# Layer 0's two attentions leave their outputs by feature, with the softmax shares applied a stage later

## The chip, the cores and the metric

One core of one Trainium2 chip runs the whole program in one launch. The metric is device time in microseconds (us): the median of three runs. TensorE does matrix products and transposes, VectorE and ScalarE work on 128 partitions, GpSimd does small vector work, and DMAs are issued by the queues of SyncE, ScalarE and GpSimd. In the profile they are PE (with PEld for its weight loads), DVE, ACT, POOL and SP; a `q` behind the name is the engine's DMA queue.

## What is computed

Two transformer layers on x, 8 samples x 512 tokens x 320 features, with a context of 8 x 64 x 192. Only layer 0 is changed. With 20 heads of 16 features:

```python
def _attn(x, ctx, wq, wk, wv, wo, bo, heads):
    q, k, v = ...                       # heads x 16 features
    sim = jnp.einsum('bhid,bhjd->bhij', q, k) * scale
    a = jax.nn.softmax(sim, axis=-1)
    out = jnp.einsum('bhij,bhjd->bhid', a, v)
    return out.transpose(0, 2, 1, 3).reshape(b, n, heads * dh) @ wo + bo
x = _attn(ln(x), ln(x), ...) + x        # self-attention
x = _attn(ln(x), context, ...) + x      # cross-attention
a, g = split(ln(x) @ ff_w1 + ff_b1); x = a * gelu(g) @ ff_w2 + ff_b2 + x
```

Everything is fp32; a product is made exact enough from rounded high and low halves (names in `_hi`, `_lo`, `_tail`).

## The kernel before

`transformer` runs one stage after another: the opening with q, k and v (to 207.5 us of the profile), `self_attention` (to 701.8), `dense_phase` with main "q", which applies the attention's output weight, adds to x, normalises and makes the queries of cross-attention (to about 852), `cross_attention` (to 1028.9), `dense_phase` with main "ff" (to 1552), and then layer 1 (to the end at 3341), whose own functions are not changed and whose dense phases already take their input by feature (`by_feature=True`, tile `attn_T`). Each stage is one block of five instruction streams held together by counting semaphores; each engine works strictly in the order written, so a wait holds everything behind it. The next stage's first loads wait for the last stores of the stage before.

**Self-attention** works in 40 groups, each of 4 heads of one sample (5 groups a sample), in 8 units `j` of PE work: two score matmuls by query for the row maxima (`natural`, L1250, tile `nat`), two transposed score matmuls (`transposed`, L1259, tile `sT`), and products with v (L1277, tile `o_ps`). The maxima are DVE's (L1391, 16 a group), the exponentials ACT's (L1325). The maxima are cut into three bf16 parts by POOL (L1362 to L1365), turned by PE (L1267, `turn_shift`), copied by ACT (L1330) and sent by SP as four small DMAs into `q_stack` (L1211). SP also loads q and k (L1196, 12 DMAs a group) and v (L1237). A finished group is in `o_ps` as 4 heads x 32 rows (16 values, the softmax sum in row 16) by 512 tokens. ACT copies it to `o_sb` (L1318), PE turns it by four transposes in unit 2 (`turn_output`, L1287), ACT copies it to `o_turned` (L1334), DVE takes 16 reciprocals (L1385), POOL multiplies (L1352), and SP stores it by token (`self_out`, L1232).

**The dense phases** go through 8 samples, each engine by the list `body`, whose steps run `ahead` samples in front. `oT` turns the loaded attention output (12 transposes a sample, L848, from `attn_nat`, loads L691 and L695); ACT and DVE split it (L949 `oT_hi`, L1012 `oT_lo`); `oproj` multiplies (L326) and DVE adds it to `x_resid` (L1016); statistics and `z` follow (L1023, L1034). By feature, as in layer 1, `attn_T` is loaded by three DMAs (L677, L680) of which the first two blocks of 128 rows are one, and `oT` is the split alone. In the q stage the loop between samples goes over the single tile of the loaded input. In "ff", PE is occupied throughout by `ff1` and `ff2` (L326, L891), with the steps of the next sample between them.

**Cross-attention** also has 40 groups, each with 64 keys: `nat` L2017, `sT` L2026, shift turn L2034, `turn_output` L2052, products L2044 on PE; exp L2084, copy of the shift rows L2089, its two DMAs L2092 and the copy `o_sb` L2098 on ACT; maxima L2156, reciprocal L2132 and multiplication L2134 on DVE; parts L2116 to L2119 on POOL, which behind each of the first groups also converts weights of the next stage (`PoolLoader`, L246 to L271) and adds the output bias to x (`EarlyBias`, L306, the first 32 groups). SP loads q (L1963, three DMAs a group), k (L1953) and v (L1973) and stores (L2000).

## Time and profile before

| what | us |
|---|---|
| median of 3 runs | 3343.64 (3338.16 to 3344.39) |
| the profiled execution, device time | 3342.7 |
| its span | 3341.0 |
| self-attention, layer 0 | 207.5 to 701.8 |
| q-dense, layer 0 | 701.8 to 852 |
| cross-attention, layer 0 | 852 to 1028.9 |
| ff-dense, layer 0 | 1028.9 to 1552 |

The span is 1.7 us shorter than the device time of the same execution. The mean granted clock of TensorE was 0.841 of full speed. A timeline row is one instruction or a run of equal ones; in brackets stands the idle time of the engine before it and what ended it.

### The profile page before, as it was taken

Reading aid. Unit: us, or ns where it says so; the run is one execution under the profiler, and the core shown is the slowest. Engines: PE = TensorE matmul, PEld = TensorE weight load, DVE = VectorE, ACT = ScalarE, POOL = GpSimd, SP = SyncE. Lnnn points to the kernel's source line nnn. Section 1 sums busy time; section 2 is a strip of 40 time slices with the busy share of each in tenths; the row PEclk is TensorE's granted clock in tenths of the full one; section 3 lists DMA queues with packets and bytes.
Section 4 is the critical chain, followed back from the end, with each engine's and each line's share of the span. In section 5 each row is a group of like instructions: output and inputs, shape, how many; then the busy total and the mean of one; then the engine's idle time right before and its main releaser. Section 6 shows DMA issues by size and latency. Waiting matters only on the chain. (4 is left out here: it accounts for less than half of the span.)

```text
span 3341.0 us, 47964 instructions
## 1 busy us (share of the span) xinstructions
PE 2936.9 (88%) x15594; PEld 1775.7 (53%) x15594; DVE 2157.7 (65%) x3834; ACT 1892.4 (57%) x3214; POOL 805.5 (24%) x1149
## 2 busy tenths in 40 slices
PE   6989999978696999998959999879978577899999
PEld 5754444457455888886731111111126342788888
DVE  5668888837453444444649999968868685444443
ACT  4328888844353232233549999989975355333322
POOL 2021221114640000000027888200003471200000
PEclk9969999989798999998975555555559898899999
DMA  8663333336762000001567557266723213010000
GB/s 228 211 166 101 106 107 103 90 80 158 165 176 46 10 10 19 9 0 38 152 173 163 128 137 164 32 90 83 97 56 96 79 45 92 26 36 18 25 17 16
DMA packets 358243, 296.57 MB, mean 89 GB/s; under 512 B 175602, under 2 KB 281914, under 8 KB 358058
## 3 DMA queue, kind: packets, MB, share of 16 engines
q1 hardware_dynamic: 347994, 273.93, 34.0%
q0 software_dynamic: 7280, 18.07, 2.1%
q10 hardware_dynamic: 2784, 2.29, 0.4%
q8 instruction: 94, 1.54, 0.2%
q14 instruction: 91, 0.75, 0.1%
HBM read 177.53 MB, written 114.52 MB: 87 GB/s over the span
## 5 line engine op out<-in xcount | busy, mean ns | idle before, releaser
L1591 PE MATMUL nat<-k_stack,q_stack 48*128 48x512 bf16 x640 | 381.0, 605 | 71.5 <-DMA k_stack<-k1w 31.1
L1391 DVE TENSOR_REDUCE neg_max<-nat 128x1 f32<-128x512 f32 x640 | 400.7, 682 | 61.3 <-PE nat L1250 61.2
L1625 DVE TENSOR_REDUCE m_all<-nat 128x1 f32<-128x512 f32 x640 | 423.3, 691 | 18.1 <-PE nat L1591 17.8
L804 POOL TENSOR_TENSOR rstd<-var_eps,neghalf 128x4 f32<-128x4 f32 x48 | 51.9, 1081 | 1588.0 <-DVE var_eps L1028 1588.0
L1645 ACT ACTIVATE nat<-nat,m_all 128x512 f32<-128x512 f32 x640 | 427.7, 2130 | 3.0 <-DVE m_all L1625 2.9
L1645 ACT ACTIVATION_READ_ACCUMULATOR nat<-nat,m_all 128x1 f32 x640 | 403.6, 1674 | 0.0
L1054 DVE SCALAR_TENSOR_TENSOR ff<-outp,bias,gel 128x512 f32<-128x512 f32 x160 | 120.1, 751 | 417.6 <-PE outp L326 417.6
L1325 ACT ACTIVATE probs<-sT 128x1024 f32<-128x1024 f32 x320 | 328.0, 1027 | 93.1 <-PE sT L1259 85.5
L968 ACT ACTIVATE gel<-outp,bias 128x512 f32<-128x512 f32 x160 | 110.0, 688 | 351.6 <-PE outp L326 351.6
L1839 ACT ACTIVATE exps<-sT 128x1024 f32<-128x1024 f32 x320 | 293.4, 1573 | 10.5 <-PE sT L1788 10.5
L972 ACT CAST ff_hi<-ff 128x512 fp32r<-128x512 f32 x160 | 99.2, 620 | 312.3 <-DVE ff L1054 312.3
L1591 PEld LDWEIGHTS nat<-k_stack,q_stack 48*128 48x128 bf16 x640 | 64.1, 102 | 387.9 <-ACT nat L1645 350.8
L1876 DVE TENSOR_SCALAR probs<-exps 128x1024 bf16<-128x1024 f32 x320 | 218.3, 692 | 67.8 <-ACT exps L1839 67.8
L1788 PE MATMUL sT<-q_stack,k_stack 51*128 51x512 bf16 x640 | 194.2, 604 | 34.6 <-DMA q_stack<-shift_rows 12.2
L1250 PE MATMUL nat<-k_stack,q_stack 48*128 48x512 f32 x640 | 200.8, 524 | 20.1 <-DMA k_stack<-k_hi 11.7
L1277 PE MATMUL o_ps<-probs,v_stack 128*32 128x256 f32 x2560 | 199.8, 394 | 1.1 <-issue 1.1
L1057 DVE TENSOR_TENSOR ff_lo<-ff,ff_hi 128x512 fp32r<-128x512 f32 x160 | 122.1, 763 | 109.7 <-ACT ff_hi L972 109.7
L1048 DVE TENSOR_TENSOR hT_lo<-h,hT_hi 128x512 fp32r<-128x512 f32 x144 | 111.6, 780 | 106.0 <-ACT hT_hi L963 105.7
L1250 PEld LDWEIGHTS nat<-k_stack,q_stack 48*128 48x128 f32 x640 | 80.0, 193 | 163.6 <-DVE neg_max L1391 129.2
L1259 PE MATMUL sT<-q_stack,k_stack 51*128 51x512 f32 x640 | 157.7, 430 | 0.5 <-ACT probs L1325 0.2
L1788 PEld LDWEIGHTS sT<-q_stack,k_stack 51*128 51x128 bf16 x640 | 34.0, 102 | 184.0 <-ACT exps L1839 165.7
L326 PE MATMUL outp<-hT_hi,Wff_hi 128*128 128x512 f32 x320 | 125.9, 393 | 4.6 <-DVE hT_lo L1048 4.6
(561 smaller groups left out, 7163.3 us busy)
## 6 DMA issues: line engine op xcount, KB each, us to landing
v<-vpad SPq DMA_DIRECT2D x64, 320.0 KB, 2.8
q_stack<-q_part SPq DMA_DIRECT2D x90, 160.0 KB, 5.8
k_stack<-k1w SPq DMA_DIRECT2D x90, 160.0 KB, 10.5
q_stack<-q_hi SPq DMA_DIRECT2D x160, 64.0 KB, 2.5
v_stack<-v SPq DMA_DIRECT2D x40, 256.0 KB, 3.2
q_stack<-q_hi SPq DMA_DIRECT2D x80, 128.0 KB, 2.8
raw<-v SPq DMA_DIRECT2D x16, 640.0 KB, 14.9
k_stack<-k_hi SPq DMA_DIRECT2D x158, 64.0 KB, 2.2
```

The costliest lines, as they stand in the source:

```text
L326: mm = pe.matmul(out, stay, move, start=(n == 0), stop=(n == len(terms) - 1))
L1250: pe.matmul(nat[(16 * n + t) % 3][:, :], q_stack[half, n % RING, pr, qt * P:(qt + 1) * P], k_stack[half, n % RING, pr, :], start=True, sto ...
L1259: mm = pe.matmul(sT[use % 2][:, ab, :], k_stack[half, n % RING, pr, kt * P:(kt + 1) * P], q_stack[half, n % RING, pr, :], start=True, stop ...
L1277: mm = pe.matmul(o_ps[VCOL * h:VCOL * h + VCOL, tok], v_stack[:, n % 2, kt, VCOL * h:VCOL * h + VCOL], probs[:, n % 2, h, kt, tok], start= ...
L1325: act.activation(probs[:, n % 2, 2 * pr:2 * pr + 2, kt, :], sT[use % 2][:, :, :], ACT.Exp, scale=DH ** -0.5).then_inc(s["a_turn_free"], 1)
L1391: dve.tensor_reduce(neg_max[:, n % 2, qt, 2 * pr + ab:2 * pr + ab + 1], nat[(16 * (n + 2) + t) % 3][:, :], AX.X, ALU.max, negate=True).the ...
L1591: pe.matmul(bank[i % NAT][:, :], q_stack[half, slot, g, pr, qt * P:(qt + 1) * P], k_stack[half, slot, g, pr, :], start=True, stop=True).th ...
L1625: dve.tensor_reduce(k.m_all[:, column(i // TILES, i % TILES)], bank[i % NAT][:, :], AX.X, ALU.max, negate=True).then_inc(s["e_max_ready"], 1)
L1645: act.activation(b[:, :], b[:, :], ACT.Exp, bias=k.m_all[:, col], accum_out=k.s_all[:, col]).then_inc(s["a_nat_free"], 1)
L1788: mm = pe.matmul(sT[u % TURNS][:, ab, :], k_stack[half, slot, g, pr, kt * P:(kt + 1) * P], q_stack[half, slot, g, pr, :], start=True, stop ...
L1839: act.activation(exps[:, u % EXPS], sT[u % TURNS][:, :, :], ACT.Exp).then_inc(s["a_turn_free"], 1)
L1876: dve.tensor_scalar(probs[:, u % KEPT], exps[:, u % EXPS], ROUND, -ROUND, ALU.add, ALU.add).then_inc(s["e_rounded"], 1)
```

## The change

In layer 0, both attentions store `o_ps` as it is: [128 x 512] per group, 4 heads x 32 rows, sums included and not divided (256 KB in place of 128 KB). `turn_output`, the second copy and the per-group reciprocal and multiplication are gone; the first copy is ACT's in self-attention and DVE's in cross-attention, into two buffers. Once a sample, SP loads the 20 rows of sums as [80 x 128], DVE inverts them, (self-attention only) POOL splits the result into halves, and SP stores these shares. The dense phases load the undivided output by heads (rows 0 to 15 of each 32): heads 0 to 7, heads 8 to 15, and heads 16 to 19 twice. New steps `scale` multiply it by the shares: in q, PE spreads the 20 shares over the features by one matmul a block into the banks that the transposes had, and DVE multiplies in place, three samples ahead; in ff, the shares are loaded broadcast to all features (8 DMAs a sample in place of 5) and DVE multiplies one sample ahead. The 12 transposes a sample are gone in both. The tile is free for the next load when `oT_lo` is done, where it was free after the transposes.

In cross-attention also: queries are loaded for two groups at once (three DMAs for two groups), the shift rows go in one DMA in place of two, POOL converts weights on every fourth group only and only those of the output and the first part of `ff_w2` (the second part is converted in the ff stage), and the bias is added in the last 32 groups in place of the first 32.

```diff
+            ahead = {"oT": 1, "oproj": 1, "stats": 1, "norm": 1, "zT": 1, "tail": -1, "scale": 1}
+            between = [[("tail", 0), *scale], oT[0:2], oT[2:], oproj[0:2], oproj[2:], [("stats", 0)], [("norm", 0)],
                        zT[0:2], zT[2:], []]
             body = []
...
+            if scale:
+                ahead["scale"] = 3
...
+                    zT[0], zT[1], oproj[1], zT[2], *scale[0:2], oproj[2], *scale[2:], oproj[3]]
...
+            if scale and main == "ff":
+                n_attn, shares = 8, sb("shares", [P, 3, TOK])
+            elif scale:
+                n_attn, shares = 5, sb("shares", [2 * HEADS, TOK], F32R)
+                spread = sb("spread", [2 * HEADS, ZCOL], F32R)
...
+                    if scale:
+                        heads = rows(attn_in, b * (QUADS * P), QUADS * P).rearrange("(h c) t -> h c t", c=VCOL)[:, 0:DH, :]
+                        loads = [(attn, heads)]
+                        if main == "ff":
+                            shared = rows(recips, b * HEADS, HEADS).unsqueeze(1).broadcast_to([HEADS, DH, TOK])
+                            loads.append((shares, shared))
+                        else:
+                            sp.dma_start(words(shares[:, :]), rows(recips, b * (2 * HEADS), 2 * HEADS)
+                                         ).then_inc(s["attn_in_loaded"], 16)
+                        for tile, src in loads:
+                            for c in range(2):
+                                sp.dma_start(tile[:, c, :], src[8 * c:8 * c + 8]).then_inc(s["attn_in_loaded"], 16)
+                            for half in range(2):
+                                sp.dma_start(tile[64 * half:64 * half + 64, 2, :], src[16:HEADS]
+                                             ).then_inc(s["attn_in_loaded"], 16)
...
+                if recips_stored:
+                    sp.wait_ge(s[recips_stored], s.before(recips_stored))
...
+                    if kind == "scale" and main != "ff":
...
+                        if m == 0:
+                            pe.wait_ge(s["attn_in_loaded"],
+                                       at["attn_in_loaded"] + b * (16 * n_attn) + 16 * n_attn)
+                        bank_free(pe, st, b)
+                        pe.matmul(bank_of(st, r)[:, :], spread[:, m * P:(m + 1) * P], shares[:, :], start=True, stop=True
+                                  ).then_inc(s[turned[st][0] + "_full"], 1)
...
+                    if kind == "scale":
...
+                        dve.tensor_tensor(attn[:, m, :], attn[:, m, :], share, ALU.mult).then_inc(s[done], 1)
...
+                    sums_of = rows(out, b * (QUADS * P), QUADS * P).rearrange("(h c) t -> h c t", c=VCOL)[:, DH, :]
+                    sp.dma_start(sums, sums_of.rearrange("h (x t) -> h x t", t=P)
+                                 ).then_inc(s["a_sums_loaded"], 16)
...
+                    wait(sp, "a_share_split", 2 * b + 2)
+                    for i, half in enumerate((share_hi, share_lo)):
+                        sp.dma_start(rows(recips, (2 * b + i) * HEADS, HEADS).rearrange("h (x t) -> h x t", t=P),
+                                     words(half)).then_inc(s["a_recip_stored"], 16)
...
+                        wait(sp, "a_o_copied", n - 1)
+                        sp.dma_start(rows(out, (n - 2) * P, P), o_sb[:, n % 2, :]).then_inc(s[f"a_o_stored{n % 2}"], 16)
+                    if exists(n - 3) and (n - 3) % QUADS == QUADS - 1:
+                        load_sums((n - 3) // QUADS)
+                    if exists(n - 6) and (n - 6) % QUADS == QUADS - 1:
+                        store_shares((n - 6) // QUADS)
                     if exists(n + 1):
                         wait(sp, "a_pv_done", n)
                         sp.dma_start(v_stack[:, (n + 1) % 2, :, :],
                                      rows(v, (n + 1) * TOK, TOK).rearrange("(t p) c -> p t c", p=P)
                                      ).then_inc(s[f"a_v_loaded{(n + 1) % 2}"], 16)
...
-                        if exists(n - 2) and j == 2:
-                            turn_output(n - 2)
...
                         wait(act, "a_pv_done", n - 1)
-                        wait(act, "a_turn_full", output_use(n - 3) + 1 if n > 2 else 0)
-                        act.copy(o_sb[:, :], o_ps[:, :]).then_inc(s["a_o_copied"], 1)
+                        wait(act, f"a_o_stored{n % 2}", 16 * (n // 2 - 1))
+                        act.copy(o_sb[:, n % 2, :], o_ps[:, :]).then_inc(s["a_o_copied"], 1)
...
-                        if exists(n - 2) and j == 2:
-                            wait(act, "a_turn_full", output_use(n - 2) + 1)
-                            wait(act, "a_o_normed", n - 3)
-                            act.copy(o_turned[:, n % 2, :], output_bank(n - 2)).then_inc(s["a_turn_free"], 1)
...
+                def split_shares(b):
+                    wait(pool, "a_recip", b + 1)
+                    wait(pool, "a_recip_stored", 32 * b)
+                    pool.tensor_copy(share_hi, shares).then_inc(s["a_share_split"], 1)
+                    wait(pool, "a_share_split", 2 * b + 1)
+                    pool.tensor_tensor(share_lo, shares, share_hi.bitcast(F32), ALU.subtract
+                                       ).then_inc(s["a_share_split"], 1)
...
-                    if n >= 4:
-                        norm(n - 4)
+                    if n > 2 * QUADS and n % QUADS == 1:
+                        split_shares(n // QUADS - 2)
...
+                def invert(b):
+                    wait(dve, "a_sums_loaded", 16 * (b + 1))
+                    wait(dve, "a_share_split", 2 * b)
+                    dve.reciprocal(shares, sums).then_inc(s["a_recip"], 1)
...
+                        if t == 8 and exists(n - 4) and (n - 4) % QUADS == QUADS - 1:
+                            invert((n - 4) // QUADS)
...
+                    wait(sp, "x_recip", b + 1)
+                    sp.dma_start(rows(recips, b * HEADS, HEADS).rearrange("h (x t) -> h x t", t=P), shares
+                                 ).then_inc(s["x_recip_stored"], 16)
...
-                    if exists(n - 1) and exists(n - 1 + RING):
+                    if exists(n - 1) and exists(n - 1 + RING) and n % 2 == 0:
                         wait(sp, "x_turn_free", uses["scores", n - 1] + 1)
-                        load_q(n - 1 + RING)
+                        load_q((n - 1 + RING) // 2)
                     if exists(n - 1) and n % PER == 0 and b - 1 + KEYS < BATCH:
+                        wait(sp, "x_turn_free", uses["scores", n - 1] + 1)
...
+                    if exists(n - 2):
+                        wait(sp, "x_o_copied", n - 1)
+                        sp.dma_start(rows(out, (n - 2) * P, P), o_sb[:, n % 2, :]).then_inc(s[f"x_o_stored{n % 2}"], 16)
+                    if exists(n - 3) and (n - 3) % PER == PER - 1:
+                        load_sums((n - 3) // PER)
+                    if exists(n - 5) and (n - 5) % PER == PER - 1:
+                        store_shares((n - 5) // PER)
...
-                    if exists(n - 2):
-                        turn_output(n - 2)
...
-                            act.dma_start(words(q_stack[QROWS:ROWS, (n + 2) % RING, pr, :]),
-                                          words(shift_sb[6 * pr:6 * pr + 6, n % 2, :])
-                                          ).then_inc(s[f"x_shift_loaded{n % 2}"], 16)
-                    if exists(n - 1):
-                        wait(act, "x_pv_done", n)
-                        wait(act, "x_o_turned", n - 1)
-                        act.copy(o_sb[:, :], o_ps[(n - 1) % 2][:, :]).then_inc(s["x_o_copied"], 1)
+                        act.dma_start(words(q_stack[QROWS:ROWS, (n + 2) % RING, :, :]), words(shift_sb[0:12, n % 2, :])
+                                      ).then_inc(s[f"x_shift_loaded{n % 2}"], 16)
...
-                    loader.turn(pool, n)
-                    if n < BATCH * TT:
-                        early.add(pool, n)
+                    if n % 4 == 3 and n // 4 <= len(loader.jobs):
+                        loader.turn(pool, n // 4)
+                    if n >= NQ - BATCH * TT:
+                        early.add(pool, n - (NQ - BATCH * TT))
...
-                def norm(n):
...
-                    dve.reciprocal(recip[:, r], o[:, :, :, DH]).then_inc(s["x_recip"], 1)
-                    wait(dve, "x_recip", n + 1)
-                    dve.tensor_tensor(o_nat[:, r], o[:, :, :, 0:DH],
-                                      recip[:, r].unsqueeze(3).broadcast_to([P, TT, 4, DH]), ALU.mult
-                                      ).then_inc(s["x_o_normed"], 1)
...
+                    wait(dve, "x_pv_done", n + 1)
+                    wait(dve, f"x_o_stored{n % 2}", 16 * (n // 2))
+                    dve.tensor_copy(o_sb[:, n % 2, :], o_ps[n % 2][:, :]).then_inc(s["x_o_copied"], 1)
+
+                def invert(b):
+                    wait(dve, "x_sums_loaded", 16 * (b + 1))
+                    wait(dve, "x_recip_stored", 16 * b)
+                    dve.reciprocal(shares, sums).then_inc(s["x_recip"], 1)
...
+            w2 = [Split(nc, s, own, "ff_w2", rows(w["ff_w2"], 0, 2 * P), over=wo)]
...
+            w2.append(Split(nc, s, own, "ff_w2", rows(w["ff_w2"], 2 * P, FF - 2 * P)))
             dense_phase(nc, s, k, 0, "ff", w["n3_g"], w["n3_b"], [w1, *w2], wo2, cross_out,
...
+                        ff_bias=(w["ff_b1"], w["ff_b2"]), next_weights=w2[1:], by_feature=True, recips=cross_shares,
```

## Rows read from the trace of the kernel before

**Rows 1.** The page: span, and busy time, share and instructions of each engine.
```profile
span 3341.0 us, 47964 instructions
...
PE 2936.9 (88%) x15594; PEld 1775.7 (53%) x15594; DVE 2157.7 (65%) x3834; ACT 1892.4 (57%) x3214; POOL 805.5 (24%) x1149
```

**Rows 2.** Windows: stretch, us, busy (x) of PE, PEld, DVE, ACT, POOL, PEclk, DMA, GB/s.
```profile
250.00:660.00 410.00, 399.42 (x3682) 168.37 (x3680) 359.14 (x603) 336.97 (x390) 78.22 (x207) 1.00 0.37 102
706.00:830.00 124.00, 104.96 (x595) 89.15 (x596) 89.19 (x195) 55.67 (x92) 44.24 (x58) 0.93 0.56 137
858.00:878.00 20.00, 13.59 (x56) 10.86 (x56) 7.85 (x12) 4.39 (x6) 13.75 (x32) 0.50 1.12 207
858.00:1010.00 152.00, 139.52 (x819) 83.53 (x820) 74.23 (x149) 73.53 (x109) 88.85 (x229) 0.89 0.71 170
1060.00:1552.00 492.00, 487.23 (x2632) 432.57 (x2632) 203.24 (x384) 145.41 (x226) 28.10 (x15) 0.99 0.05 10
```

**Rows 3.** Timeline of PE in self-attention of layer 0: start, us, what, xcount.
```profile
452.77 0.50 PE L1250 MATMUL nat<-k_stack,q_stack 48*128 48x512 f32 x2
...
453.65 0.63 PE L1287 MATMUL sT<-ident,o_sb 128*128 128x128 f32 x4
...
454.77 0.51 PE L1250 MATMUL nat<-k_stack,q_stack 48*128 48x512 f32 x2
...
456.01 0.54 PE L1250 MATMUL nat<-k_stack,q_stack 48*128 48x512 f32 x2
```

**Rows 4.** Timeline of DVE in the same stretch.
```profile
450.41 0.24 DVE L1385 RECIPROCAL recip<-o_turned 128x16 f32<-128x16 f32 x1
...
461.98 0.24 DVE L1385 RECIPROCAL recip<-o_turned 128x16 f32<-128x16 f32 x1
```

**Rows 5.** Groups, one period of self-attention: busy us, mean ns, idle before and releaser.
```profile
L1391 DVE TENSOR_REDUCE neg_max<-nat 128x1 f32<-128x512 f32 x17 | 10.7, 681 | 1.4 <-PE nat L1250 1.4
```

**Rows 6.** Timeline of all engines at the end of self-attention.
```profile
696.41 0.59 ACT L1318 COPY o_sb<-o_ps 128x512 f32<-128x512 f32 x1 [2.60 <-PE o_ps L1277]
...
701.84 2.09 SPq L691 DMA_DIRECT2D attn_nat<-self_out  x4
```

**Rows 7.** Timeline of DVE in the q-dense stage of layer 0.
```profile
749.98 0.49 DVE L1016 TENSOR_TENSOR x_resid<-x_resid,oproj 128x320 f32 x1 [0.31 <-PE oproj L326]
...
755.04 0.69 DVE L1012 TENSOR_TENSOR oT_lo<-oT,oT_hi 128x512 fp32r<-128x512 f32 x1 [0.17 <-ACT oT_hi L949]
755.65 2.66 DVE L1034 TENSOR_SCALAR z<-x_resid,mv,rstd 128x320 f32 x4
...
765.37 0.49 DVE L1016 TENSOR_TENSOR x_resid<-x_resid,oproj 128x320 f32 x1 [0.32 <-PE oproj L326]
```

**Rows 8.** DMA issues: xcount, KB each, median us from issue to landing.
```profile
attn_T<-self_out_T SPq DMA_DIRECT2D x8, 512.0 KB, 4.2
```

**Rows 9.** GB/s in 40 slices of 2826 to 2836 us, layer 1's ff-dense loading.
```profile
GB/s 0 0 57 106 57 369 385 377 426 393 393 271 189 102 26 1 1 2 2 1 1 0 1 1 2 7 6 4 4 9 100 139 126 96 70 80 41 79 109 254
```

**Rows 10.** Timeline of all engines in cross-attention of layer 0.
```profile
969.08 1.03 ACT L2084 ACTIVATE probs<-sT 128x1024 f32<-128x1024 f32 x1
...
969.30 0.66 PE L2052 MATMUL o_ps<-ident,o_sb 128*128 128x128 f32 x4
...
970.58 1.39 ACTq L2092 DMA_DIRECT2D q_stack<-shift_sb  x2
...
972.07 0.59 ACT L2098 COPY o_sb<-o_ps 128x512 f32<-128x512 f32 x1 [1.52 <-issue]
...
972.56 1.03 ACT L2084 ACTIVATE probs<-sT 128x1024 f32<-128x1024 f32 x1
```

**Rows 11.** Groups in the first 40 us of cross-attention.
```profile
L306 POOL TENSOR_TENSOR x_resid<-x_resid,early_bias 128x320 f32<-128x320 f32 x7 | 6.0, 857 | 0.0
```

**Rows 12.** Timeline of PE in the ff-dense stage of layer 0.
```profile
1132.52 1.04 PE L848 MATMUL misc<-ident,attn_nat 128*128 128x128 f32 x8
...
1138.81 0.60 PE L848 MATMUL misc<-ident,attn_nat 128*128 128x128 f32 x4
```

More of the change, by code:

```diff
@@ L523, in dense_phase @@
         has_o = wo is not None
+        scale = [("scale", m) for m in range(3)] if recips is not None else []
         oT, oproj, zT = ([(x, m) for m in range(n)] for x, n in (("oT", 3), ("oproj", TT), ("zT", 3)))
@@ L1904, in cross_attention @@
         shift_sb = sb("shift_sb", [32, 2, TOK], F32R)
-        o_sb, o_nat = sb("o_sb", [P, TOK]), sb("o_nat", [P, 2, TT, 4, DH])
-        recip = sb("recip", [P, 2, TT, 4])
+        o_sb = sb("o_sb", [P, 2, TOK])
+        sums, shares = (k.m_all[0:TT * HEADS, P * i:P * i + P] for i in range(2, 4))
         loader = PoolLoader(nc, s, ctx, next_weights, 160)
@@ L2113, in _ @@
                     wait(pool, "x_turn_full", uses["shift", n - 1] + 1 if n else 0)
-                    mine = neg_max[:, n % 4]
-                    one, two, three = (parts[:, :, i:12:3] for i in range(3))
+                    mine, left = (x.rearrange("p t (a r) -> p t a r", a=2) for x in (neg_max[:, n % 4], rest[:, :, :]))
+                    columns = parts[:, :, 0:12].rearrange("p t (a i r) -> p t a i r", a=2, i=3)
+                    one, two, three = (columns[:, :, :, i, :] for i in range(3))
@@ L2159, in _ @@
                     if exists(n - 2):
-                        norm(n - 2)
+                        copy(n - 2)
+                    if exists(n - 4) and (n - 4) % PER == PER - 1:
+                        invert((n - 4) // PER)
+                invert(BATCH - 1)
         for name, n in counts.items():
             s.passed(name, n)
-        s.retire(counts)
+        s.retire([name for name in counts if name != "x_recip_stored"])
         loader.passed()
```

187 lines of the change are left out of this document (88 added, 99 removed).

## The prediction

> **What bounds the kernel now.** I read the page first: PE is busy for 88% of the span [rows 1]. So the question at each stage is whether PE is the engine that ends last there, and the windows answer it [rows 2]. Self-attention has PE busy 399.42 of 410 us at full clock, with DVE behind it at 359.14. In ff-dense PE works 487.23 of 492 us. In q-dense it works 104.96 of 124, so something else takes turns with it. In cross-attention it works 139.52 of 152, at a clock of 0.50 in the first 20 us. What PE loses in the first, the third and the last of these stages shortens them; in q-dense the loop between samples has to be walked. Layer 1 (1552 to 3341 us) is untouched.
>
> **Self-attention.** PE loses four transposes a group. Units 2 and 3 hold the same work but for them: they begin at 452.77, 454.77 and 456.01, so 2.00 against 1.24 us, a difference of 0.76 [rows 3]. The period is 11.57 us, from one reciprocal on DVE to the next [rows 4]. The next engine is DVE: 17 maxima take 10.7 us, so the group's 16 take 10.1, and its idle time of 1.4 us is all spent waiting for PE's scores [rows 5]. So the period can't fall under 10.1 (1.5 saved), and at the other end it stays at 11.57, if SP with its 18 DMAs a group can go no faster. I take PE's own 0.76, which still leaves DVE 0.7 us of slack: 38 steady groups x 0.76 = 29 us. ACT loses one copy and POOL a multiplication, both hidden. DVE's 16-column reciprocal of 0.24 us [rows 4] becomes one of 128 columns a sample. No row shows that; it lies between the 0.24 of 16 columns and eight times this, 1.9. I take 0.9, half of it in DVE's slack: 8 of them cost 4 us. POOL's split lies beside PE's work. The end grows: today 5.4 us pass from the last `o_sb` copy to the next stage's first load [rows 6]; then come a store, a load of sums, an inversion, a split and two stores, a transfer more, but no transposes: +3. **Self-attention: -29 + 4 + 3 = -22** (0 to -35).
>
> **q-dense.** The period is 15.4 us: the last add of one sample starts at 749.98, of the next at 765.37 [rows 7]. What counts is a new loop. The tile is now free when `oT_lo` is done, at 755.73 (755.04 + 0.69) [rows 7], 5.2 us behind the end of the last add (750.47). Only then may SP load the sample after, and PE waits in order for it before `oproj` 2 and 3. From the first `scale` to the end of the last add I count one matmul, two rounds of 8 oproj matmuls and their adds, 3.7 us. The loop is 5.2 + D + 3.7 with D the time from free tile to loaded tile. DVE has 89.19 us of work in 124 [rows 2], 11.1 a period, and gets three multiplications like `oT_lo`'s 0.69: 13.2, less than 15.4. PE loses 12 transposes and gets 3 matmuls. So the period stays near 15.4 unless D is over 6.5.
>
> D has two ends. Layer 1 loads the same 768 KB by feature in three DMAs and its large one lands in 4.2 us [rows 8]; with two more issues before the last lands, D is 5.5, and the loop of 14.4 stays hidden. The other end follows from the shape: every load of the trace with this many bytes has 128 rows as its outermost dimension, these have 8, 8, 4 and 4 heads. If each is spread over no more DMA engines than it has heads, four engines get 16 + 16 + 16 + 16 = 64 rows of 2 KB. All 16 engines together reach 426 GB/s [rows 9], so one moves 27 GB/s and a row takes 0.077 us: 4.9 us, with 2.4 us of fixed time (4.2 less 768 KB at 426 GB/s) and one issue in front, D = 7.9. The loop is then 16.8 us. I take this end: rows 8 is a row for a transfer of another shape, and this is the step on which my number hangs. 7 rounds x 1.4 = 10; the first load lands 2.4 later and its multiplications stand ahead of the first split (+2); PE's lost transposes in the warm-up give back 2. **q-dense: +12** (-3 with the early end; up to +20).
>
> The Trainium skill, "DMA: Bandwidth & Descriptors", the section on why a DMA increments its semaphore by 16, says that the engines used are the largest number up to 16 that divides the slowest dimension of both sides, and that from a hardware queue they are the lowest-numbered ones. By that the loads would use 8, 8, 4 and 4 engines and q-dense would be at +12; by the row of layer 1 alone it would be at -3. No row of this profile shows the number of engines of a transfer, so it stays open here.
>
> **Cross-attention.** The period between exponentials is 3.48 us (969.08 to 972.56). Two cycles are this long. PE has no gap and has the transposes in it, 0.66 as modelled, with 0.58 from their start to that of the products. ACT's is exp 1.03, shift copy 0.56, two DMA issues 1.39 and `o_sb` copy 0.59, 3.5 in all [rows 10]. The change cuts both: ACT loses the copy and one issue (to about 2.3) and PE the 0.58, to 2.90. DVE exchanges 0.68 for a copy of about 0.69; it has 74.23 of 152 us [rows 2]. From the 12th group on, 28 groups x 0.58 = 16 us. In the first 11 groups POOL sets the pace, busy 13.75 of 20 us [rows 2], and the bias additions there, 7 in 40 us at 0.86 [rows 11], move to the end, where POOL has room; but DMA is overfull there too (share 1.12 [rows 2]), so I count only 5 us. SP issues 22 DMAs a sample for 28. The end is longer by a transfer, +3. **Cross-attention: -18** (-8 if DMA, at a share of 0.71 before [rows 2], holds the period near 3.2; -27 if the start gains fully).
>
> **ff-dense.** 8 + 4 transposes a sample lie in a full PE: four more take 1.04 - 0.60 = 0.44 us, 0.11 each, and 12 are 1.31 [rows 12]. Seven samples in the steady part: -9.2. DVE's three multiplications have cover: it works 203.24 of 492 us; if that were gone they would cost 2 us a sample. The POOL work moved here (POOL 28.10 of 492 [rows 2]) is hidden until `ff2` needs the weights in the first sample. The first sample has no cover: with few engines 128 rows x 0.077 = 9.9 us against some 5 today, and multiplications before the split: +7. **ff-dense: -2** (-9 with the early end).
>
> **Sum.** -22 + 12 - 18 - 2 = -30. It is made against the profiled execution, 3342.7 us, which is 0.9 under the median: 3312.7, or 3313.6 by the median. I say 3313.
>
> **Rivals.** (1) *The head-wise loads land early.* For it: rows 8, and the DMA share of 0.56 in q-dense. Against it: their shape. Then -22 - 3 - 18 - 9 = -52: 3291. (2) *Something other than PE holds the attentions.* In self-attention SP issues 18 DMAs in 11.57 us and waits for the maxima's shift in between, and DVE's new inversion waits for a load of sums in the middle of its maxima; if the period stays at 11.3, 38 x 0.5 = 19 us of the gain are gone: 3332. For it: DVE is at 88% [rows 2]. Against it: its idle time is all PE's doing. (3) *Slower than before: the clock falls in q-dense.* PE waits at every sample for a late load there, with 85% busy and a clock of 0.93 now [rows 2]. At 0.50, as in 858 to 878, its 105 x 0.93 = 98 us of full-speed work take 195: +71 on the 124, 41 us over before, 3384. It decides once the low level covers more than 30/71 = 0.42 of the stage. Against it: self-attention leaves the clock at 1.00, and a PE at 80% does not look like the idle starts at which 0.50 stands. (4) *The stages give back at their ends what they gain*: the chain of last store, load of sums, inversion and store of shares stands at two ends, where today 5.4 us pass [rows 6]; were it 15 us longer than I count at each, the time would be 3343, no change. Against it: its transfers are 40 KB and less, and rows 8 has 4.2 us for 512 KB.
>
> **How the numbers follow.** My case has 0.50 (its own range 3300 to 3325), rival 1 has 0.24, rival 2 has 0.14, rival 3 has 0.06, rival 4 has 0.06. The range leaves out the clock, and the deepest gains of self-attention together with early loads: 3284 to 3336. About 0.2%, 6.7 us, is what a measurement can tell from no change. My case, the early loads and most of rival 2 lie beyond it: faster 0.88, same 0.05, slower 0.07.
>
> **What would show it.** Right: starts of unit 2 and 3 in self-attention alike, period 10.8; a q-dense period of 16.8 with PE idle for `attn_T`; exponentials 2.9 apart; layer-0 ff samples without L848 on `attn_nat`. Wrong: a landing of `attn_T` in layer 0 near 4 us (then 3291), a self-attention period that stays over 11 with DVE or SP before it, a granted clock at 0.50 within q-dense.

## The result, and the profile after

The changed kernel takes 3377.15 us (median of four runs, 3369.85 to 3382.74) against 3343.68 us, the median of four runs of the kernel before: a ratio of 1.0102 (95% interval 1.0076 to 1.0129), 33 us slower, where 3313 had been forecast. Its profiled execution has a span of 3380.3 us. The page and the windows that answer to [rows 1] and [rows 2]:

```profile
span 3380.3 us, 46635 instructions
...
PE 2928.0 (87%) x15106; PEld 1756.9 (52%) x15106; DVE 2206.2 (65%) x3820; ACT 1853.1 (55%) x3134; POOL 789.0 (23%) x1125
```

```profile
250.00:640.00 390.00, 381.27 (x3571) 155.41 (x3571) 363.70 (x577) 321.56 (x357) 60.77 (x183) 1.00 0.42 123
700.00:830.00 130.00, 95.42 (x392) 74.05 (x392) 84.76 (x169) 45.86 (x75) 39.76 (x49) 0.78 0.35 110
940.00:960.00 20.00, 20.00 (x70) 10.49 (x70) 6.79 (x10) 5.92 (x8) 9.08 (x24) 0.52 0.76 170
1100.00:1580.00 480.00, 474.44 (x2520) 420.43 (x2521) 217.34 (x399) 146.61 (x226) 44.70 (x31) 0.99 0.07 22
```

PE is busy for 9 us less and the kernel is 39 us longer in this execution. The loss shows in the clock column: q-dense, at 0.93 before, is at 0.78 (the second of these rows), and cross-attention has stretches in which PE is busy without a gap at a clock near 0.50 (the third). The stages, each from the first load of one to the first load of the next:

| us | before | after | difference | forecast |
|---|---|---|---|---|
| opening, up to self-attention's first load | 200.2 | 196.0 | -4.2 | 0 |
| self-attention | 501.7 | 477.6 | -24.0 | -22 |
| q-dense | 150.8 | 206.3 | +55.5 | +12 |
| cross-attention | 176.2 | 184.6 | +8.4 | -18 |
| ff-dense | 522.7 | 523.9 | +1.1 | -2 |
| layer 1 | 1789.4 | 1791.9 | +2.5 | 0 |

The mark of 207.5 us at which the table ahead of the prediction begins self-attention lies 7.3 us behind that stage's first load. Between profiles of the same code there are a few us: layer 1 takes 1788.2 to 1793.5 us in all the runs of this document, and the unchanged self-attention of e6 below takes 500.1.

**Self-attention** gained what was forecast. ACT's `o_sb` copies in the timeline of the changed kernel are 10.89 us apart, for 11.57 [rows 4]:

```profile
446.04 0.58 ACT L1373 COPY o_sb<-o_ps 128x512 f32<-128x512 f32 x1
...
456.93 0.58 ACT L1373 COPY o_sb<-o_ps 128x512 f32<-128x512 f32 x1
```

The end of the stage, in the timeline of all engines, is 8.4 us from the last copy to the next stage's first load (5.4 before [rows 6]), and the reciprocal of 80 x 128 takes 0.95 us:

```profile
665.22 0.58 ACT L1373 COPY o_sb<-o_ps 128x512 f32<-128x512 f32 x1 [3.82 <-PE o_ps L1342]
...
670.48 0.95 DVE L1433 RECIPROCAL m_all<-m_all 80x128 f32<-80x128 f32 x1 [26.49 <-DMA m_all<-self_out]
...
673.65 0.30 SPq L692 DMA_DIRECT2D shares<-self_shares  x1
```

**q-dense** is where the time went. Its period, last add to last add, is 23.13 us for 15.4 [rows 7]; DVE's timeline:

```profile
746.71 0.49 DVE L1074 TENSOR_TENSOR x_resid<-x_resid,oproj 128x320 f32 x1 [1.87 <-PE oproj L326]
...
769.84 0.49 DVE L1074 TENSOR_TENSOR x_resid<-x_resid,oproj 128x320 f32 x1 [1.86 <-PE oproj L326]
```

The queue of SP asks for the next sample at 752.62, right behind `oT_lo`, and PE stands idle for 4.60 us before its first `scale` matmul, which starts at 763.09. These are SP's row and then PE's:

```profile
752.62 0.33 SPq L692 DMA_DIRECT2D shares<-self_shares  x1
```

```profile
753.68 0.31 PE L326 MATMUL oproj<-o_w_lo,oT_hi 128*128 128x320 f32 x1
753.82 0.31 PE L326 MATMUL oproj<-o_w_hi,oT_lo 128*128 128x320 f32 x1
...
763.09 1.02 PE L887 MATMUL oT<-shares,spread 40*128 40x512 f32 x2 [4.60 <-DMA attn_T<-self_out]
...
764.46 0.47 PE L326 MATMUL oproj<-o_w_lo,oT_hi 128*128 128x320 f32 x1
764.73 0.47 PE L326 MATMUL oproj<-o_w_hi,oT_lo 128*128 128x320 f32 x1
```

So the time D of the prediction, from asking to loaded, is 10.5 us here, and 9.7 to 10.5 over the six loads of the steady part. Behind the wait the same pair of oproj matmuls is spaced by 0.27 us where it was 0.14 before the wait: the clock's lower level, 1.2 for 2.4 GHz. The loop reads 5.4 + 10.5 + 7.2 = 23.1.

The seven periods of the stage are 21.0, 22.7, 23.1, 22.9, 22.7, 22.8 and, with no load left in it, 14.9 us: together 42.8 us more than before. Another 11.4 us are lost ahead of them, from the stage's first load to the last add of the first sample: 29.3 us (673.65 to 702.99), for 17.9 before (701.84 to 719.73). The end is 1.3 us longer. DVE's rows, after and before:

```profile
702.99 0.49 DVE L1074 TENSOR_TENSOR x_resid<-x_resid,oproj 128x320 f32<-128x320 f32 x1 [1.74 <-PE oproj L326]
```

```profile
719.73 0.49 DVE L1016 TENSOR_TENSOR x_resid<-x_resid,oproj 128x320 f32<-128x320 f32 x1 [0.68 <-PE oproj L326]
```

**Cross-attention** takes 12.4 us more in the part that was to gain most. From the 12th exponential to the 40th and last it takes 108.8 us, for 96.4 before. Up to the 12th it gains 5.3 us, counted from the stage's first load, and its end is 1.3 us longer. ACT's rows, after and before:

```profile
945.88 1.02 ACT L2145 ACTIVATE probs<-sT 128x1024 f32<-128x1024 f32 x1 [3.67 <-PE sT L2095]
...
1054.70 1.02 ACT L2145 ACTIVATE probs<-sT 128x1024 f32<-128x1024 f32 x1 [2.09 <-PE sT L2095]
```

```profile
923.84 1.02 ACT L2084 ACTIVATE probs<-sT 128x1024 f32<-128x1024 f32 x1
...
1020.29 1.02 ACT L2084 ACTIVATE probs<-sT 128x1024 f32<-128x1024 f32 x1
```

**ff-dense** begins worse and runs better. Its first `ff1` product starts 40.9 us behind the stage's first load at 1064.57 in the changed kernel, and 33.0 us behind 1028.87 in the kernel before; what follows is 483.0 against 489.8 us. After, then before:

```profile
1105.46 0.79 PE L326 MATMUL outp<-hT_hi,w_hi 128*128 128x512 f32 x1 [3.71 <-DVE hT_lo L1106]
```

```profile
1061.83 0.80 PE L326 MATMUL outp<-hT_hi,w_hi 128*128 128x512 f32 x1 [3.42 <-DVE hT_lo L1048]
```

### The profile page after: what moved, and what is told of

It is laid out like the page before. It is cut to its first block and busy times, and to the rows that moved or that the text cites. A ratio compares the mean times of both kernels' runs of the same rounds, so it can differ in the third digit from the quotient of the medians.

```text
span 3380.3 us, 46635 instructions
## 1 busy us (share of the span) xinstructions
PE 2928.0 (87%) x15106; PEld 1756.9 (52%) x15106; DVE 2206.2 (65%) x3820; ACT 1853.1 (55%) x3134; POOL 789.0 (23%) x1125
## 5 line engine op out<-in xcount | busy, mean ns | idle before, releaser
L990 ACT CAST oT_hi<-attn_T 128x512 fp32r<-128x512 f32 x96 | 56.0, 618 | 151.2 <-PE oproj L326 83.8
L326 PE MATMUL outp<-hT_hi,w_hi 128*128 128x512 f32 x320 | 126.0, 394 | 4.9 <-DVE hT_lo L1106 3.7
```

The source lines that it names most:

```text
L326: mm = pe.matmul(out, stay, move, start=(n == 0), stop=(n == len(terms) - 1))
```

## The experiments

The expectations name their rival theories by letters. In the text below "theory D" is one of these, and D alone is the time of a load, from asking to loaded.

**1. Is it the shape of the load?** e1 loads contiguous blocks in q-dense (not the right rows, so the result is another one):

```diff
-    sp.dma_start(tile[:, c, :], src[8 * c:8 * c + 8])            # 8 heads x 16 rows
+    sp.dma_start(tile[:, c, :], rows(attn_in, b * 640 + 128 * c, 128))
```

> The changed kernel, but the q-dense stage loads its attention input as contiguous blocks of 128, 128, 64 and 64 rows in place of the gather by heads: the same bytes in the same number of DMAs, though not the right rows, so the result of layer 0 is another one. Theory A (the load by heads is slow because of its shape, and PE's waiting for it costs the clock too): the time from the free tile to the loaded one falls from 10.4 us to about 5.5, the period of the stage from 23.1 to 15 or 16, the stage from 206 us to 155 or less, the total by 45 to 50 us against the changed kernel, to some 3325. Theory B (any load into the one tile is that late, since it is asked for only when the tile is free and has five DMAs): the period stays over 21 and the total over 3360.

Measured: 3331.44 us (3325.68 to 3340.88), ratio to before 0.9975 (0.9962 to 0.9987); q-dense 162.5 us. In its timeline the load is asked for at 736.43 and the matmul that waits for it starts at 742.92, D = 6.5:

```profile
736.43 0.34 SPq L692 DMA_DIRECT2D shares<-self_shares  x1
...
742.92 0.72 PE L895 MATMUL oT<-shares,spread 40*128 40x512 f32 x2 [0.63 <-DMA attn_T<-self_out]
```

The period is 17.2 us. Theory B (over 21 us) is out. Theory A has the direction and most of the size: it had a D of about 5.5, a period of 15 or 16, a stage of 155 us or less and a total of some 3325. The transfers in 40 slices of 12 us, of the changed kernel from 752 and of e1 from 753, so that both loads are asked for some 0.7 us behind the first slice's start; first the busy share of the 16 DMA engines in tenths, then GB/s:

```profile
DMA  0092389894444454458999999997789874332222
GB/s 0 0 222 51 137 341 427 338 290 96 120 143 164 171 184 157 171 205 335 369 341 341 369 403 396 389 280 205 191 205 253 218 184 130 109 116 102 109 96 102
```

```profile
DMA  0097289899914999997799999999988610000000
GB/s 0 0 137 102 51 341 461 355 266 195 79 34 150 369 382 410 417 369 157 253 369 416 389 410 417 396 410 382 376 314 273 184 41 0 0 0 0 0 0 0
```

By heads, the mean busy share of the DMA engines falls to 4 and 5 tenths, at 96 to 205 GB/s, for nine slices, 2.7 us, in the middle of the load. It rises again behind the first stores of the queries (asked for from 756.44). In blocks the load runs at 7 to 9 tenths but for three slices. Gaps between the rows could do that as well as the outermost dimension of 8 and 4, so e8 keeps gaps and takes the small dimension away:

```diff
-    sp.dma_start(tile[:, c, :], src[8 * c:8 * c + 8])
+    sp.dma_start(tile[:, c, :], rows(attn_in, b * 640 + 256 * c, 256).rearrange("(p two) t -> p two t", two=2)[:, 0, :])
```

> The changed kernel, but q-dense loads every second row of the attention output: rows that don't lie together, as in the load by heads, but with 128 (or 64) rows as the outermost dimension where the load by heads has 8 (or 4) heads of 16. It leaves out the right rows, so layer 0's result is another one. If the outermost dimension decides how many DMA engines work, the load takes 6.5 us as with the contiguous blocks, the stage about 163 us, the total about 3331. If it is the gaps between the rows that make the load by heads slow, it takes 10.5 us, the stage 206 us and the total 3377.

```profile
739.46 0.34 SPq L692 DMA_DIRECT2D shares<-self_shares  x1
...
746.78 0.73 PE L897 MATMUL oT<-shares,spread 40*128 40x512 f32 x2 [1.45 <-DMA attn_T<-self_out]
```

D = 7.3, q-dense 169.4 us, the total 3336.75 (3325.01 to 3346.79), ratio 0.9977 (0.9964 to 0.9989). Over the six loads of the steady part D is 6.1 to 7.4 us in blocks (mean 6.6), 6.2 to 7.3 with gaps (7.0) and 9.7 to 10.5 by heads (10.0). So the gaps cost some 0.4 us (0.8 in the two loads shown), and the small outermost dimension some 3. The rule of the Trainium skill that the prediction weighed ("DMA: Bandwidth & Descriptors", "Why a DMA increments its semaphore by 16 and not by 1") fits this. The number of engines of a transfer is in no row here; what the rows show is the mean busy share of 0.4 to 0.5.

**2. Hide the load.** e2 gives q-dense two tiles and two semaphores, used in turn (SP's loop over the samples is written out for this):

```diff
+    attn2 = sb("attn_T2", [P, 3, TOK])
-    load_attn(b + early, b + (early - 1))     # waits for the split of the sample before
+    load_attn(b + early, b + (early - 2))     # of the one before that
```

> The changed kernel with two tiles for the attention input and the shares in the q-dense stage, so that the load of the next sample is asked for a sample earlier; loads by heads as they are. Theory A and B both say that the load is then hidden: period about 15.5, stage about 155 us, total about 3325. Theory C (not the wait for the load but the added matmuls and multiplications in the order of PE and DVE set the period): it stays near 20 and the total over 3355.

Measured: 3330.94 us (3321.73 to 3348.97), ratio 0.9966 (0.9950 to 0.9983). q-dense takes 165.9 us, 40 less than in the changed kernel. In its steady part the clock is 1.00 and DVE is busy for 85% of the window:

```profile
709.00:813.00 104.00, 83.35 (x438) 64.05 (x438) 88.87 (x177) 48.51 (x80) 43.73 (x54) 1.00 0.44 140
```

But the period is 17.3 us, not 15.5. DVE's rows, then PE's:

```profile
747.55 0.49 DVE L1091 TENSOR_TENSOR x_resid<-x_resid,oproj 128x320 f32 x1 [0.47 <-PE oproj L327]
...
764.85 0.49 DVE L1091 TENSOR_TENSOR x_resid<-x_resid,oproj 128x320 f32 x1 [0.49 <-PE oproj L327]
```

```profile
745.54 0.49 PE L904 MATMUL oT<-shares,spread 40*128 40x512 f32 x1 [1.32 <-DVE attn_T L1081]
...
752.62 0.44 PE L327 MATMUL outp<-hT_hi,q_hi 128*64 128x512 f32 x1 [1.57 <-DVE st_lo L1145]
```

With the load hidden, 1.9 us a sample of loss remain. PE stands 1.32 us before the third `scale` matmul, which needs the bank that DVE drains behind its `hT_lo`, and 1.57 us before the third q product. So theory C has a part, a small one. In e1 the period is 17.2 us too: with D at 6.5 the load no longer sets it alone.

**3. Cross-attention: which edit makes PE wait?** In the changed kernel the shift rows are PE's one large wait in the steady part of the stage, 15.3 us in 10 waits (view of the waits, from 895 to 1060); in the kernel before they were 2.2 us:

```profile
PE sT L2095 <- DMA q_stack<-shift_sb: 15.3, 10, 4.6
```

In PE's timeline one such wait of 2.27 us is followed by 24 us at the low clock, where a group takes 5.3 us; at 965.35 the `sT` matmuls are back at 0.68:

```profile
936.57 1.11 PE L2086 MATMUL nat<-k_stack,q_stack 96*128 96x128 f32 x8
939.95 0.74 PE L2095 MATMUL sT<-q_stack,k_stack 102*128 102x512 f32 x2 [2.27 <-DMA q_stack<-shift_sb]
...
942.91 1.97 PE L2086 MATMUL nat<-k_stack,q_stack 96*128 96x128 f32 x8
...
948.21 1.97 PE L2086 MATMUL nat<-k_stack,q_stack 96*128 96x128 f32 x8
...
965.35 0.68 PE L2095 MATMUL sT<-q_stack,k_stack 102*128 102x512 f32 x2
```

e3 takes back the loads for two groups, at the start of the stage as well as in its steady part:

```diff
-    def load_q(pair):     # 3 DMAs of 256 KB for two groups
+    def load_q(n):        # 3 DMAs of 128 KB a group
```

> The changed kernel with the queries of cross-attention loaded for one group at a time, three DMAs a group, as in the kernel before. Theory D (the loads for two groups, 256 KB each, stand before the shift rows on the DMA engines, PE waits for these and its clock drops after the wait): PE's 15.3 us of waiting for shift rows fall under 4, the stage goes from 184.6 to about 160 us, the total from 3377 to about 3352. Theory E (the clock drops in cross-attention because of the slow q-dense stage before it, or PE's own load): the stage stays within 5 us of 184.6.

```profile
PE sT L2094 <- DMA q_stack<-shift_sb: 5.2, 6, 1.7
```

Measured: the wait falls to 5.2 us, cross-attention to 166.3 us, the total to 3364.26 (3362.97 to 3368.76), ratio 1.0072 (1.0056 to 1.0089). Theory D had under 4 us, about 160 and about 3352, so it has the direction and part of the size; and the total by itself shows nothing, for the changed kernel taken once more (e11 below) has the same ratio, 1.0072. The table below settles the waits. e4 takes back the single shift DMA, and with it the order of the maxima in it:

```diff
-    act.dma_start(words(q_stack[QROWS:ROWS, (n + 2) % RING, :, :]), words(shift_sb[0:12, n % 2, :]))
+    for pr in range(2):
+        act.dma_start(words(q_stack[QROWS:ROWS, (n + 2) % RING, pr, :]), words(shift_sb[6 * pr:6 * pr + 6, n % 2, :]))
```

> The changed kernel with the shift rows of cross-attention sent as two DMAs of 6 rows, as in the kernel before. Theory F (one DMA of 12 rows lands later than two of 6): PE's waiting for shift rows falls from 15.3 us to under 5 and the total by 15 us or more. Theory D (they wait behind the loads of queries in either form): the wait stays at 10 to 20 us and the total within 8 us of the changed kernel's 3377.

Measured: 3379.05 us (3373.41 to 3392.42), ratio 1.0121 (1.0094 to 1.0149). The same within the spread, with 24.3 us of waiting for shift rows: theory F is out, the one DMA is no worse than two. All the profiles together, for this stage:

| queries loaded by | kernels | PE's waits for shift rows, us | first exponential behind the stage's first load, us | stage, us |
|---|---|---|---|---|
| 256 KB | changed, e1, e2, e4, e6, e8, e11 | 15.3, 16.3, 13.5, 24.3, 17.9, 15.6, 19.4 | 22.0 to 25.0 | 184.6, 169.1, 186.7, 178.1, 168.1, 178.1, 170.4 |
| 128 KB | e3, e5, e9, e10, e12 | 5.2, 3.7, 2.2, 2.4, 6.4 | 16.2 to 18.0 | 166.3, 159.2, 163.5, 164.2, 152.0 |
| 128 KB, stage as before | before, e7 | 2.2, 1.4 | 19.8, 19.1 | 176.2, 177.5 |

The waits go with the size of the loads in every kernel. That the shift rows, which are asked for on ACT's queue, stand behind these loads on the DMA engines is the likely reason, but no row shows their order. The bigger loads have a second price: the first exponential comes 4 to 9 us later. Of e3's 18 us, 8 lie ahead of the 12th exponential. The slow q-dense stage of theory E is out as well: in e1, e2 and e8 q-dense takes 162.5 to 169.4 us, and cross-attention still 169.1 to 186.7. How long the stage takes does not follow the sum of the waits: e2 has the fewest of the first row and the longest stage, with a mean clock of 0.74 from 856 to 1022 us.

**4. The parts alone.** e6 has only cross-attention and ff-dense of the change, e7 only self-attention and q-dense, with e2's two tiles:

```diff
# e6
-    self_attention(nc, s, k, q0, k0, v0, self_out, self_shares, [wq, wo], w["o1_b"])
+    self_attention_before(nc, s, k, q0, k0, v0, self_out, [wq, wo], w["o1_b"])
# e7
-    cross_attention(nc, s, k, q20, k20, v20, cross_out, cross_shares, [wo2, *w2], w["o2_b"])
+    cross_attention_before(nc, s, k, q20, k20, v20, cross_out, [wo2, *w2], w["o2_b"])
```

> Only the part of the change in cross-attention and ff-dense; self-attention and q-dense as in the kernel before. If cross-attention's loss is its own (queries by two groups before the shift rows), its stage takes 175 to 187 us against 176.2 and ff-dense 524 against 522.7: total 3340 to 3353, within 0.3% of before. If the drop of the clock in cross-attention comes from the slow q-dense stage before it, the stage takes 155 to 165 us and the total is 3322 to 3330.

> Only the part in self-attention and q-dense, with two tiles for the attention input; cross-attention and ff-dense as in the kernel before. Self-attention -27, q-dense +15 (a period of 17.3 against 15.4 and the later start), cross-attention 176 and ff-dense 523 as before: 3329, about 12 us faster. Rival (what self-attention gains comes back in q-dense's start and in layer 1): within 3 us of before.

e6: 3335.44 us (3330.29 to 3351.61), ratio 0.9982 (0.9968 to 0.9995); cross-attention 168.1 us, with 17.9 us of waiting for shift rows behind a q-dense stage of 151.5 us. This lies between the two forecasts: the waits are cross-attention's own, and what they cost differs from run to run (its spread is 21 us). e7: 3337.05 us (3332.35 to 3343.72), ratio 0.9977 (0.9966 to 0.9988), with 480.7, 165.0, 177.5 and 523.7 us in the four stages. That is 6 us under the kernel before, between the forecast of 12 and the rival's 3 at most. The profiled run, 4 us slower than the median, has self-attention 6 us over its forecast of -27 and layer 1 4 us longer (1793.5 for 1789.4), which is the same code.

**5. Both repairs, and what is left.** e5 is e2 and e3 together.

> The changed kernel with both repairs: two tiles for the attention input in q-dense, and queries of cross-attention loaded for one group at a time. Theory: the two losses lie in different stages and add up; q-dense 166 us and cross-attention 166 us as in the two runs alone, self-attention 467, together some 13 to 20 us under the double-tile kernel's 3331: 3311 to 3318, faster than the kernel before by about 25 us. Rival (cross-attention's clock depends on the stage before it, so with a full q-dense it drops anyway): cross-attention stays near 185 us and the total near 3330.

Measured: 3322.70 us (3316.79 to 3333.05), ratio 0.9943 (0.9928 to 0.9958), 5 us over the forecast range, with q-dense at 166.2 us and cross-attention at 159.2 in the profiled run. The rival (cross-attention near 185) is out, and the ratio is lower than with either repair alone, though its interval still touches e2's. Against the kernel before, cross-attention gains its 17 us ahead of the 12th exponential; from there to the last it takes 96.2 us for 96.4. DVE, PE and ACT of e5 show the next stall:

```profile
907.99 0.95 DVE L2209 RECIPROCAL m_all<-m_all 80x128 f32<-80x128 f32 x1 [3.96 <-DMA m_all<-cross_out]
```

```profile
909.63 1.64 PE L2103 MATMUL nat<-k_stack,q_stack 96*128 96x128 f32 x8 [2.42 <-DVE neg_max L2229]
```

```profile
902.86 1.03 ACT L2162 ACTIVATE probs<-sT 128x1024 f32<-128x1024 f32 x1 [1.42 <-PE sT L2112]
...
905.76 1.02 ACT L2162 ACTIVATE probs<-sT 128x1024 f32<-128x1024 f32 x1 [1.42 <-PE sT L2112]
...
912.27 1.02 ACT L2162 ACTIVATE probs<-sT 128x1024 f32<-128x1024 f32 x1 [5.03 <-PE sT L2112]
...
917.57 1.02 ACT L2162 ACTIVATE probs<-sT 128x1024 f32<-128x1024 f32 x1 [3.83 <-PE sT L2112]
```

DVE stands 3.96 us for the sums ahead of its maxima, PE 2.42 us behind it, and the exponentials, 2.90 us apart until then, come at 6.5 and 5.3. e9 puts the inversion one group later, and the store of the shares too:

```diff
-    if exists(n - 4) and (n - 4) % PER == PER - 1:
-        invert((n - 4) // PER)
+    if exists(n - 5) and (n - 5) % PER == PER - 1:
+        invert((n - 5) // PER)
```

> The kernel with both repairs and, in cross-attention, the inversion of the sums one group later on DVE (and the store of the shares one group later on SP). Theory G: with both repairs what is left of cross-attention's stalls comes from DVE waiting 4 us for the sums ahead of its maxima, PE waiting 2.4 us behind it, and the clock then at 0.50 for three groups of 5.3 us. Without that wait the two long stretches at 5.3 go, cross-attention falls from 159 to 145 to 152 us and the total from 3323 to 3308 to 3316. Rival H: the clock falls by itself whatever PE waits for; the 5.3 us stretches stay and the stage is 155 to 165 us.

Measured: 3319.05 us (3310.31 to 3320.39), ratio 0.9908 (0.9888 to 0.9928). PE's waits for the maxima are gone (0.4 us), but stretches at 5.3 us were still there in the profiled run (163.5 us for the stage, where theory G had 145 to 152), behind waits of 1.4 and 1.5 us for others. Theories G and H each have a part; how often the clock falls is not settled.

e10 asks what the 1.9 us a sample in q-dense are. It is e5 with multiplications that cover 8 of 512 columns:

```diff
-    dve.tensor_tensor(mine, mine, share, ALU.mult)
+    dve.tensor_tensor(mine[:, 0:8], mine[:, 0:8], share[:, 0:8], ALU.mult)
```

> The kernel with both repairs, where the three multiplications by the shares in q-dense cover 8 of 512 columns; it leaves the other columns undivided, so its result is another one. Theory I: DVE's three full multiplications (2.1 us a sample) are on the path that sets q-dense's period of 17.3 us; without them it is 15.2 to 15.5 and the stage 150 to 153 us for 166, the total 13 to 16 us under 3323. Rival J (PE's added matmuls and their order set the period): it stays over 16.8 and the stage over 162.

```profile
746.24 0.49 DVE L1091 TENSOR_TENSOR x_resid<-x_resid,oproj 128x320 f32 x1 [1.32 <-PE oproj L327]
...
763.01 0.49 DVE L1091 TENSOR_TENSOR x_resid<-x_resid,oproj 128x320 f32 x1 [1.33 <-PE oproj L327]
```

Measured: 3317.13 us (3314.38 to 3321.72), ratio 0.9918 (0.9897 to 0.9939); the period is 16.77 us, the stage 162.1. Theory I is out, and rival J holds but for 0.03 us. The multiplications are 0.5 of the 1.9 us; the order of PE's queue is the larger suspect, so e12 moves the third scale step behind the last product, on top of e9:

```diff
-    zT[2], *scale[0:2], oproj[2], *scale[2:], oproj[3]]
+    zT[2], *scale[0:2], oproj[2], oproj[3], *scale[2:]]
```

> The kernel with both repairs and the later inversion, and in q-dense the third scale step moved behind the last oproj step, so that PE does not stand before that product until VectorE has drained the bank of the first scale step. Theory K (the order of PE's queue, 1.3 us of waiting at the third scale matmul, is the larger part of what is left of q-dense's loss): the period falls from 17.3 to about 16.0 us, the stage from 165 to about 156 us, the total from 3319 to about 3310. Rival L (VectorE's own chain sets the period, it only gets the same work in another order): the period stays over 16.9 and the total within 4 us of 3319.

```profile
727.07 0.88 DVE L1091 TENSOR_TENSOR x_resid<-x_resid,oproj 128x320 f32 x2
...
743.40 0.88 DVE L1091 TENSOR_TENSOR x_resid<-x_resid,oproj 128x320 f32 x2
```

The period is 16.33 us (743.40 - 727.07 in DVE's timeline), the stage 162.2: the wait was worth 1.0 us a sample, between theory K's forecast and rival L's. The stage gained only 2.9 us for K's 9: its seven periods are 4.4 us shorter together, and its end, behind the last add, is 1.9 us longer. The total is 3308.86 us (3304.47 to 3313.08), ratio 0.9905 (0.9888 to 0.9921). Against e9's ratio of 0.9908, taken on another chip, the total can't tell the two apart, and e12's profiled run owes most of its lead over e9's to cross-attention (152.0 us for 163.5), which the edit leaves alone. Against the kernel before, both are 0.9% faster. They are the best complete versions here: the change with two tiles in q-dense, single-group query loads and the later inversion.

Last, the changed kernel itself again:

> The changed kernel itself once more, on the chip of the two kernels above. Every theory: 3370 to 3383, q-dense at 206 us; what varies from run to run is how long cross-attention spends at the low clock.

Measured: 3368.65 us (3366.83 to 3374.92), ratio 1.0072 (1.0050 to 1.0094), 1 us under the forecast range, with 203.5 us in q-dense and 170.4 in cross-attention, 14 less than in the first profile. So +8.4 for cross-attention in the first table is one draw from a range of about -6 to +8; with e1, e2 and e8, which have the same code there, -7 to +10.

## Why the prediction was wrong

**Self-attention: right.** The transposes were worth 0.68 us a group for 0.76, the end cost +3.0 as forecast, and the reciprocal is 0.95 us for 0.9. -24 for -22. DVE kept slack, as forecast: from 300 to 600 us its waits for PE's scores are 17.6 us, for 37.7 before.

**q-dense: right mechanism, badly sized, and this step alone turns the sign.** The forecast loop of 5.2 + 7.9 + 3.7 = 16.8 us measured 5.4 + 10.5 + 7.2 = 23.1. Three terms were short, in the loop shown:
- *D = 7.9.* The loads in the warm-up, with no stores of queries beside them, took 8.6 and 8.9 us (asked for at 687.54, matmul at 696.15). Within the loop the stores of the queries are asked for 4 us behind the load, and D was 10.5. The working had counted the load's own rows alone. That the stores make the difference is likely; no run took them away. The working also has a slip: its 4.2 us are the landing of a transfer of 512 KB [rows 8], from which it takes the time of 768 KB. With 512 KB its fixed time is 3.0 us and its D 8.5, near the warm-up's.
- *From scale to the last add, 3.7.* At full clock it is 5.2 us (e1: 742.92 to 748.13, the end of the last add). The text had counted one matmul and two rounds of products; all three scale matmuls lie in this stretch, and the third waits until DVE has drained the first one's bank, 0.62 us in e1 and 1.32 in e2.
- *The clock.* Another 2.0 us a sample (7.2 for e1's 5.2): PE, made to wait 3.9 to 4.6 us a sample, ran the products behind the wait at the low level. Rival 3 named this mechanism and the place, and had it at 0.06; "a PE at 80% does not look like the idle starts" was the sentence that failed. The stage's mean clock was 0.76, where it was 0.90 in the kernel before and in e1 and e2, not the 0.50 that the rival priced. If the clock has only the levels 0.5 and 1, a mean of 0.76 is the low one for 0.48 of the stage, an estimate, and that is over the 0.42 at which the rival was to decide. But 3384 is near the result by luck, by another sum: most of the loss is the waiting itself.

Together with 0.2 ahead of the asking these are 6.3 us in the loop shown. Over the stage the difference of +55.5 and +12 is 43.5 us: some 33 in the seven periods (+42.8 for +10), 9 ahead of the first sample's last add, where the second load is waited for in the same way (+11.4 for some +2), and 1.3 at the end. e1 and e2 take 44 and 40 us of the stage back. "So the period stays near 15.4 unless D is over 6.5" was wrong by itself, too: with D hidden it is 17.3. Of these 1.9 us, 0.5 go with the multiplications (e10) and 1.0 with the third scale step (e12). No run has both edits, so it is not shown that the two add up; if they do, 0.4 is left open.

**Cross-attention: the step that failed is "From the 12th group on, 28 groups x 0.58 = 16 us".** An undisturbed group did fall to 2.90 us as forecast (902.86 to 905.76 in e5), but these 28 groups cost 12.4 us in place of gaining 16. The shift rows are now due in 2 groups of 2.9 us and not of 3.48, and with loads of 256 KB beside them PE waits 15.3 us for them, where the text had costed this edit at nothing, beside the gain on SP's queue. And a wait can be followed by 10 to 27 us at the low clock, 2.4 us a group, which no term held. e3 shows the first cause, e5 the second one's other source, DVE's wait for the sums, which rival 2 had named for self-attention, where it did not come. The start gained 5.3 us for 5, and the end cost 1.3 for 3.

**ff-dense: right in kind.** Late first product +7.9 for +7; steady part -6.8 for -9.2.

Rivals 2 and 4 did not come: the period of self-attention is 10.89 us, and the two ends are 3.0 and 1.3 us longer.

Rival 1, the early loads, had 0.24 and is what e1 builds in q-dense: it had 3291, and e1 measured 3331, because neither 17.2 us a sample (the stage is at +12 for -3) nor cross-attention's waits (-7 for -18) were in it, and e1 leaves ff-dense its loads by heads (+1 for -9). A load that no row resembled was priced by arithmetic on bytes, and the total hung on it; the range should have reached to the other side for that one term.

## What to carry to other kernels

Before a tile's release is moved later, walk the whole loop (release, load, first use, release) with every wait in order, and take the load's time with the other traffic of that moment; if the loop is within a few us of the period, take two tiles first. A gather whose outermost dimension is small took 10.0 us here (8 and 4 heads), where the same bytes with 128 rows outermost took 7.0. Loads made twice as big to save issues came with longer waits for what is small and urgent, and with a later first use at the stage's start. A wait of 2 us on PE can cost the clock behind it as well, so a stage that never lets PE wait can beat one with less PE work.

## What the runs showed that was not expected

- The clock can fall behind a short wait inside a busy stage: behind 2.27 us of waiting in cross-attention PE ran 24 us at half speed, and 5.3 us a group in place of 2.9. The kernel before, with PE full at 3.48 us a group, had a clock of 1.00 from 920 to 1020 us. Waits of 0.7 to 1.5 us were sometimes followed by a fall and sometimes not, and the same code spent from 169 to 187 us in this stage.
- The spread of runs was larger in some of these kernels: 3321.73 to 3348.97 us in the ten runs of e2, where nineteen of the kernel before beside them stay within 3338 to 3352.
- Rows of 2 KB with gaps between them cost only some 0.4 us more than contiguous ones in a load of 768 KB (mean D of 7.0 for 6.6).
